# The spatial and channel attention maps and the gated fusion built as one stage

## What is computed

```python
def cga_fusion(a, y, P):
    init = a + y
    pooled = init.mean((2, 3))
    mid = jax.nn.relu(pooled @ P['ca_w1'].T + P['ca_b1'])
    cattn = (mid @ P['ca_w2'].T + P['ca_b2'])[:, :, None, None]
    savg = init.mean(1, keepdims=True)
    smax = init.max(1, keepdims=True)
    sattn = rconv(jnp.concatenate([savg, smax], 1), P['sa_w'], P['sa_b'])          # 7x7, reflected edges
    pattn = jnp.broadcast_to(cattn + sattn, init.shape)
    gate = jax.nn.sigmoid(rconv(jnp.concatenate([init, pattn], 1), P['pg_w'], P['pg_b'], groups=C))   # 7x7
    out = init + gate * a + (1.0 - gate) * y
    return jnp.einsum('oc,bchw->bohw', P['op_w'], out) + P['op_b'][None, :, None, None]
```

## Time and profile before

| | us |
|---|---|
| median of 3 runs | 2468.71 |
| lowest and highest run | 2462.86, 2470.36 |
| time of the profiled execution | 2474.21 |
| its span in the profile | 2472.4 |
| PE busy in the span | 2127.1 (86%) |
| DVE busy | 1446.8 (59%) |
| ACT busy | 1151.8 (47%) |
| mean DMA rate over the span | 165 GB/s |

### The profile page before, as it was taken

How to read it: one execution, slowest core, us unless ns; L and a number is a source line. 1 busy time by engine, 2 the same in 40 slices (tenths; PEclk the granted TensorE clock), 3 DMA queues, 4 the chain that set the end, 5 groups by cost and what they waited for, 6 DMA issues and landing times. The chain is left out here.

```text
span 2472.4 us, 69200 instructions
## 1 busy us (share of the span) xinstructions
PE 2127.1 (86%) x25034; PEld 1270.3 (51%) x25034; DVE 1446.8 (59%) x2613; ACT 1151.8 (47%) x2290; POOL 527.2 (21%) x910
## 2 busy tenths in 40 slices
PE   7579949988998799999969999999993887788887
PEld 3345427866786233333326666666661776233333
DVE  4335511111112577777747888888872666588887
ACT  4336623222222588888852322323220222577776
POOL 7520005100200000000006565565641010000000
PEclk9779959999999899999979999999996999899999
DMA  6999989777762677787745555555534896344443
GB/s 152 254 246 260 255 272 318 251 245 253 265 250 88 124 147 150 141 154 140 149 82 101 110 108 103 113 102 106 112 74 130 244 282 215 94 112 108 112 107 84
DMA packets 545522, 408.62 MB, mean 165 GB/s; under 512 B 362057, under 2 KB 496897, under 8 KB 542055
## 3 DMA queue, kind: packets, MB, share of 16 engines
q1 hardware_dynamic: 463158, 359.48, 56.1%
q10 hardware_dynamic: 76128, 22.48, 4.4%
q0 software_dynamic: 6128, 25.11, 4.1%
HBM read 234.72 MB, written 175.79 MB: 166 GB/s over the span
## 5 line engine op out<-in xcount | busy, mean ns | idle before, releaser
L618 PE MATMUL gate_ps<-room 64*64 64x289 f32 x6144 | 390.3, 411 | 31.1 <-issue 23.0
L618 PEld LDWEIGHTS gate_ps<-room 64*64 64x64 f32 x6144 | 311.1, 134 | 111.4 <-issue 46.4
L679 DVE TENSOR_TENSOR gate_out<-gate_gelu,gate_ps 128x578 f32<-128x578 f32 x96 | 72.2, 756 | 376.7 <-PE gate_ps L618 327.2
L973 ACT CAST mix_h<-mix_bank 96x512 f16<-96x512 f32 x512 | 267.6, 592 | 10.4 <-PE mix_bank L924 6.5
L656 ACT ACTIVATE gate_gelu<-gate_ps 128x578 f32<-128x578 f32 x96 | 62.7, 653 | 301.5 <-PE gate_ps L618 279.8
L1058 DVE TENSOR_SCALAR mix_hb<-mix_h,mix_b1q 96x1024 f16<-96x1024 f16 x256 | 122.7, 479 | 98.1 <-ACT mix_h L973 98.1
L924 PE MATMUL mix_bank<-mix_xq,mix_w1q 112*96 112x512 fp8e5 x512 | 143.0, 381 | 34.3 <-ACT mix_h L973 23.0
L1068 DVE CAST mix_hq<-mix_hb 96x2048 fp8e5<-96x2048 f16 x128 | 156.6, 1223 | 22.1 <-DVE mix_hb L1058 20.3
L292 DVE COPY exp_out<-exp_y 128x384 f32<-128x384 f32 x192 | 102.2, 566 | 110.2 <-DMA y<-exp_out 55.2
L255 PE MATMUL exp_y<-exp_win,exp_xb 48*128 48x192 f32 x1024 | 117.4, 367 | 54.0 <-DVE exp_out L292 34.1
L2068 PE MATMUL fus_bank<-fus_xt,fus_taps 64*32 64x256 f32 x3840 | 116.7, 387 | 37.7 <-DMA fus_shift<-gate_shift 21.0
(11 more groups left out here) (237 smaller groups left out, 4141.2 us busy)
## 6 DMA issues: line engine op xcount, KB each, us to landing
y<-exp_out SPq DMA_DIRECT2D x64, 816.0 KB, 12.2
room<-y SPq DMA_DIRECT2D x24, 2176.0 KB, 17.1
g<-gate_out SPq DMA_DIRECT2D x48, 578.0 KB, 4.6
room<-g SPq DMA_DIRECT2D x31, 816.0 KB, 7.2
wav_strips<-xp SPq DMA_DIRECT2D x96, 204.0 KB, 3.5
init<-wav_init SPq DMA_DIRECT2D x48, 272.0 KB, 2.3
fus_init<-init SPq DMA_DIRECT2D x48, 272.0 KB, 8.5
xp<-mix_xn SPq DMA_DIRECT2D x124, 102.0 KB, 2.8
```

Source lines behind the costliest of these rows:

```text
L618: mm = pe.matmul(banks(a, v)[64 * g:64 * (g + 1), r], wt[q][64 * r:64 * (r + 1), 2 * a + g, n, :], src, start=n == 0, stop=n == 3)
L973: act.copy(h16[at.pair][:, m, h, :], bank[(2 * m + h) % len(bank)][0:HID, :]).then_inc(h16_ready, 1)
```

## The change

The two functions become one, `attention_and_fusion`, with one set of tiles and no barrier in between.

- SP issues, after the six mirroring copies, a wait for them to land (`mirrored`), then for each slot the loads of `fus_xt` and `fus_init`, then `fus_bias`; only then it waits for the shift and the map and stores them, waits for these stores (`map_out`), and loads `fus_spatial` and `fus_shift`.
- ACT loads its table first, waits for `mirrored`, issues the three slots' loads of `fus_taps` and `fus_xt`, and then does the five evictions of the attention.
- DVE clears behind `add_corners` and ahead of the sums and shifts; POOL clears from the stage's start.
- PE goes from the attention's products straight into the loop of the fusion, and waits for `consts_in` only ahead of each pair's map part. The wait stands inside the loop.
- The gates, outputs and differences of the fusion become slices of one tile `late`, and the attention's mean and maximum, band and padded maps are views of the same memory, in front of it. Two PSUM banks hold the attention's results beside the six of the fusion (three of the four small ones share a bank).

```diff
-def attention_maps(nc, t):
+def attention_and_fusion(nc, t, bases):
...
+        late = k.sb("late", [128, 2 * SLOTS + 1, 2, 2 * Q])
+        gate, out, diff = [late[:, u] for u in S], [late[:, SLOTS + u] for u in S], late[:, 2 * SLOTS]
+        flat = late[:, :, :, :].rearrange("p n h q -> p (n h q)")
+        maps = flat[:, 0:4 * Q].rearrange("p (n e b j) -> p n e b j", n=2, e=2, b=B)
+        band = flat[:, 4 * Q:4 * Q + 2 * TAPS * H].rearrange("p (n y) -> p n y", y=H)
...
             def _(sp):
...
-                        sp.dma_start(t["init"][:, to], t["init"][:, at]).then_inc(stored, 16)
+                        sp.dma_start(t["init"][:, to], t["init"][:, at]).then_inc(mirrored, 16)
+                sp.wait_ge(mirrored, 16 * 2 * EDGE)
+                for u in S:
+                    sp.wait_ge(lines_cleared[u], 2)
+                    load_lines(sp, 0, u, 0)
+                    load_pair(0, u)
+                sp.dma_start(bias[:, :], t["pg_b"].partition_broadcast(128)).then_inc(consts_in, 16)
                 sp.wait_ge(shift_ready, 1)
...
+                sp.wait_ge(map_out, 16 * (2 + 2 * EDGE))
+
+                sp.wait_ge(map_cleared, 2)
+                for r in range(2):
+                    sp.dma_start(spatial[64 * r:64 * r + KF].rearrange("p g b x -> p g (b x)"),
+                                 tiles(t["spatial"][64 * r:64 * r + 1])).then_inc(consts_in, 16)
+                sp.dma_start(shift[:, :, :], t["gate_shift"].partition_broadcast(128)).then_inc(consts_in, 16)
...
             def _(pe):
-                pe.wait_ge(consts_in, 64)
                 with pe.Fori(0, N) as i:
...
                         pe.wait_ge(added, c + 1)
+                        pe.wait_ge(consts_in, 64)
                         pe.sem_inc(pe_turn, 1)
...
                 load_act_tables(nc, act, SIGMOID)
                 act.sem_inc(gated, SLOTS)
+                act.wait_ge(mirrored, 16 * 2 * EDGE)
                 for u in S:
                     act.wait_ge(taps_cleared[u], 2)
                     load_taps(act, 0, u)
                     act.wait_ge(lines_cleared[u], 2)
                     load_lines(act, 0, u, 1)
+                act.wait_ge(pooled_done, 1)
+                act.activation(pooled[:, :], ps_p[0:C, 0:B], ACT.Copy, scale=1.0 / HW).then_inc(pooled_ready, 1)
...
                 clear(dve, slice(32, 64))
+                att_chain.link(dve.tensor_reduce(sums[:, :], pg_taps[:, :, :], AX.X, ALU.add))
...
-        attention_maps(nc, t)
-        fusion(nc, t, room)
+        attention_and_fusion(nc, t, room)
```

More of the change, by code:

```diff
@@ L1964, in fusion @@
-def fusion(nc, t, bases):
+def attention_and_fusion(nc, t, bases):
     SLOTS = 3
@@ L2055, in _ @@
             def _(pe):
-                pe.wait_ge(consts_in, 64)
+                pe.wait_ge(att_in, 176)
+                for b in range(B):
+                    mm = pe.matmul(ps_p[0:C, b:b + 1], row_parts[:, :, b], ones[:, 0:1], start=True, stop=True)
+                mm.then_inc(pooled_done, 1)
+                pe.wait_ge(ready, 1)
+                for j in range(2):
+                    for dx in range(TAPS):
+                        n = j * TAPS + dx
+                        mm = pe.matmul(ps_s[:, :], band[:, n, :], padded[:, B * j:B * (j + 1), dx:dx + W],
+                                       start=n == 0, stop=n == 2 * TAPS - 1)
+                mm.then_inc(conv_done, 1)
+                pe.wait_ge(pooled_ready, 1)
+                pe.matmul(ps_m[0:MID, 0:B], w1[:, :], pooled[:, :], start=True, stop=True).then_inc(mid_done, 1)
+                pe.wait_ge(mid_ready, 1)
+                for j in range(2):
+                    mm = pe.matmul(ps_c[0:GROUP, B * j:B * (j + 1)], w2[:, j, :], mid[:, :], start=True, stop=True)
+                mm.then_inc(cattn_done, 1)
                 with pe.Fori(0, N) as i:
@@ L2134, in _, with inner @@
                 chain = Chain(dve, step, 3 * SLOTS)
-                clear(dve, slice(32, 64))
+                att_chain = Chain(dve, att_step, 0)
+                dve.memset(cor[:, :, :, :], 0.0).then_inc(cleared, 1)
+                dve.wait_ge(att_in, 176)
+                def inner(j):
+                    return padded[:, B * j:B * (j + 1), EDGE:EDGE + W].rearrange("p b (j e) -> p e b j", e=2)
+                att_chain.mark(dve.tensor_scalar(inner(0), maps[:, 0], 1.0 / C, None, ALU.mult))
+                att_chain.link(dve.tensor_copy(inner(1), maps[:, 1]))
+                reflect_columns(dve, padded)
+                dve.wait_ge(bands_in, 80)
+                add_corners(dve, band, cor).then_inc(ready, 1)
+                clear(dve, slice(32, 64))
+                att_chain.link(dve.tensor_reduce(sums[:, :], pg_taps[:, :, :], AX.X, ALU.add))
+                dve.wait_ge(cattn_ready, 1)
+                att_chain.link(dve.tensor_scalar(own_shift[:, :], cattn[:, 0, :], sums[:, 0:1], pg_b[:, :], ALU.mult, ALU.add))
+                dve.scalar_tensor_tensor(out=own_shift[:, :], in0=cattn[:, 1, :], scalar=sums[:, 1:2], in1=own_shift[:, :],
+                                         op0=ALU.mult, op1=ALU.add).then_inc(shift_ready, 1)
+                dve.wait_ge(map_ready, 1)
+                for e in range(2):
+                    dve.tensor_copy(smap[:, e, :, 0:2], smap[:, e, :, 4 - e:2 - e:-1])
+                    x = dve.tensor_copy(smap[:, e, :, S0 + 2:S0 + 4], smap[:, e, :, S0 + 1 - e:S0 - 1 - e:-1])
+                x.then_inc(edged, 1)
                 dve.sem_inc(fused, SLOTS)
```

169 lines of the change are left out of this document (55 added, 114 removed).

## The result

The changed kernel takes 2454.39 us in the median of 5 runs (2450.46 to 2456.98); the kernel before, 2468.71 (2462.86 to 2470.70). The ratio is 0.9946, with a 95% interval of 0.9925 to 0.9967. In two later groups of runs, each on one chip together with the kernel before, it gave ratios of 0.9942 (0.9919 to 0.9964) and 0.9926 (0.9899 to 0.9954).

What follows compares the result with a forecast made beforehand. The border was taken as bound by a chain: map, stores, barrier, clears, loads. `gates(3)` 14.6 us earlier less 0.3 for the added wait gave 14.3; the 2468.71 median became 2454.5 us, range 2446 to 2463.

Steps and rivals of the forecast that it cites:

- Clears and slot loads move ahead by 21.1: Stage border: DVE's clears start 21.1 us earlier, covered by the filter; first slot load from 1895.05 to about 1874.0.
- The map's way through DRAM: Between filter and fusion: map store lands behind SP's slot loads at 1898.2, constants in at 1903.0 (bounds 1901.7 and 1908.5).
- the 20 that I gave as a sign: Sign at the stage border: the map's last stores issued by 1891, with the filter starting at 1871.0 before.
- `gates(0)` 10.7 earlier: First pair's gates at 1907.3 against 1918.01: constants at 1903.0, then map part 4.1 us at slow clock, plus 0.2.
- Pairs 1 to 3: Fusion's pairs after the first: 22.1 us instead of 26.0, 19.6 at PE's pace plus 2.5 of issue gaps.
- The own part of pair 0 off the path: Fusion start: PE's own part no longer waits for constants, follows attention at 1886 and takes some 5 us off the path.
- rival C: DMA sets the fusion's pace and takes the gain back: together 6 us earlier, 2462.5 us; chance 0.24.
- The body: Fusion's pairs 4 to 23, 7.25 us each: no gain and no loss.
- The added wait: Wait for constants in PE's fusion loop, 24 times at 0.03 us: 0.7 in all, 0.3 us lost after hiding.
- Rival B: Map's store served in turns with the loads, landed at 1891.5; constants at 1896, some 22 us gained, 2447; chance 0.20.
- Rival D: More PE waits in the fusion's body drop its clock; outweighs the gain from five such pairs, seven give 2476; chance 0.06.

Runs made afterwards that it cites:

- the map first: Changed kernel with SP issuing only slot 0's loads ahead of the map's stores, slots 1 and 2 after the map's loads: 2445.89 us (0.9900), again 2445.72 (0.9918).
- PE kept busy: Kernel with only slot 0's SP loads ahead of the map's stores, plus 32 unread PE products ahead of the fusion loop: 2447.33 us (ratio 0.9937).
- PE's wait on top: Changed kernel with PE waiting for the constants once, ahead of the fusion loop: 2457.12 us (0.9947), again 2454.71 (0.9970).

## Why the prediction was right, and where it was not

**The forecast** was 2454.5 us, 14.3 less on the profiled execution. From F to the last gates the profiles give 14.2 less, the medians 14.3. That it fits to a tenth is luck. The other two profiles of the changed kernel give 11.5 and 14.3 less, the medians of the other two groups 13.3 and 18.1, and the parts miss by up to 1.3 us in ways that cancel.

**Clears and slot loads move ahead by 21.1.** They moved by 21.0 (from 24.04 to 3.08 behind F), covered by the filter. That took 14.84 us for its 28 products against 14.19 before, within the 13.95 to 15.21 of the other profiles. The taps and lines of slot 2 were in by about 26 after F (POOL's `fus_whole` of slot 2, which waits for them, ran at 1889.63), as the 22.7 us from the rate of 205 GB/s said. One cover was used that I had set at nothing: with GpSimd clearing at the same time, DVE's copy into the padded maps took 2.21 us in place of 0.42. Afterwards DVE still had to wait 0.60 us for the band's corners, so the filter started no later.

**The map's way through DRAM.** Stores landed by 28.1 after F (27.2 forecast), map part at 32.5 (32.0). The number was right, the reason at best in part: I had let the stores land behind SP's slot loads *in the queue*. Two things differ. SP was held longer in issuing the slot loads than I had it: the map was stored at 19.9 behind F in place of 17.5 and its last row issued by 22.0, past the 20 that I gave as a sign. And a queue of their own gained 0.6 to 1.9 us of the 7.0 that the absence of the loads gained. The crowd on the DMA engines is the likely cause of the rest; how it divides between crowd and order stays open, as said with that experiment. The Trainium skill, "DMA: Bandwidth & Descriptors", says in its section "Issuing engines are not separate DMA queues" that DMAs of all engines run on the same 16 DMA engines. The 5.2 us of a 2.1 KB row in its own queue agree with it, and do not prove it.

**`gates(0)` 10.7 earlier**: measured 10.3. The slow clock of the map part (4.1 forecast) was 3.99.

**Pairs 1 to 3**: `gates(3)` 14.6 earlier was forecast, 13.3 came: 0.4 were missing at `gates(0)`, and the three pairs took 23.0 us in place of 22.1. The gaps that the profile puts down to issue kept 2.4 us (1.27 and 1.11 in pair 2), as the 2.5 that I took. That PE had no instructions there is my reading of them; the profile shows only that nothing else was waited for. PE stood so in the own part of pair 0 too, for 3.55 us, at no cost, since the map was later. With the map first, where the DMA share was 0.19 in that stretch, the same 160 products ran through in 4.66.

**The own part of pair 0 off the path.** I counted it into the sum in full. It brings 2.6 to 4.5 us at `gates(0)` and 4.5 to 5.1 at `gates(3)`. What is left of it at the end is open: 0 to 0.8 us by the traces, the 6.7 us between the medians by the times of the group that ran both. If the traces are right, this is where the working, not the number, was wrong: the body, which waits for its loads, takes PE's lead back, as rival C had it. What does reach the end is how early the DMAs have their work: the early loads bring 9 of the 14 us.

**The body**: neither gain nor loss, and 0.9 us was seen, under its scatter. *The added wait*: the 0.03 us each came from no row, and nine waits in one place cost nothing that shows.

**Rival B** (map not held up) came near in the experiment that took the loads away: constants by 25.9 after F. **Rival D** (slow clock in the body) came in part. The changed kernel's second profile had three pairs of 10.7 to 11.1 us, each with an own part of about 6.26 us behind a wait of 2.3 to 2.7 us for its lines, with a mean clock of 0.97 in the body (above), and the latest last gates of its three, 206.6. The third profile had one such pair, the first none, the kernel before one. Three is short of the five pairs at which it would have decided.

Left open is why with the map first the last gates are 4 us or more earlier although `gates(0)` was hardly earlier in the version with PE kept busy. That the DMAs idle less between the slot loads and the first gates would explain it. The view by stretches agrees in size. Over the first 100 us from F the three profiles of the changed kernel have a mean rate of 221, 221 and 225 GB/s, the three with the map first 234, 234 and 230. That is 0.5 to 1.3 MB more moved by then, an estimate of 2 to 5 us at the 267 GB/s of the body. It was not tried by itself. By the same count the two profiles with PE's wait on top (215 and 211) are 2 to 5 us behind, though their last gates are not.

## What to carry to other kernels

When two stages meet, look at which engine idles on each side; here DMA idled beside the filter and PE beside the loads, and laying one over the other gave what the longer chain allowed. In a loop that waits for its loads, count an early start in DMA work first: the loads that started earlier brought 9 of the 14 us. Of PE time moved off the path, 5 us here, it is not settled whether anything reached the end, so test it in the end time and do not take it over from the first gates. A small round trip through DRAM that others wait for should go when few bulk loads are in flight; here its landing took 0.9 us behind the last issue when nearly alone and 6.1 in the crowd, and a queue of its own saved 2 us at most.

## What was unexpected of the hardware

A 2.1 KB store in GpSimd's queue, behind one store of 272 KB, took 5.2 us to land while bulk loads of two other queues were in flight. PE stood for 3.55 us in the middle of a run of 160 products, waiting for nothing that the profile shows, with the DMAs busy (share 0.73). With a share of 0.19 it did not stand there at all. A DVE copy of 128x512 took 2.21 us beside a GpSimd memset, 0.42 without.
